# Flamingo layer with top-2 experts on one core: where the first expert tiles' rows are loaded, and three small edits around the blocks' boundary

## The reference

```python
x = x + tanh(g_xattn) * attention(layernorm(x), ctx, ctx)      # 16 heads of 16, causal
f = layernorm(x).reshape(-1, 256)
logits = f @ Wr + br                                           # 8 experts
weights = softmax(where(logits >= second_largest, logits, -inf))
h = gelu(einsum('td,edh->eth', f, W1) + b1)                    # 256 -> 1024
y = einsum('eth,ehd->etd', h, W2) + b2                         # 1024 -> 256
x = x + tanh(g_ffn) * einsum('etd,te->td', y, weights)
```

## Time and profile before

| | us |
|---|---|
| median of 3 runs | 907.57 (907.29 to 908.5) |
| the profiled execution | 904.24 |
| its span, first to last instruction | 902.5 |
| TensorE busy | 797.3 |
| first product of block 2 | 470.36 |

### The profile page before, as it was taken

How to read it: one execution, slowest core, us unless ns; L and a number is a source line. 1 busy time by engine, 2 the same in 40 slices (tenths; PEclk the granted TensorE clock), 3 DMA queues, 4 the chain that set the end, 5 groups by cost and what they waited for, 6 DMA issues and landing times. The chain is left out here.

```text
span 902.5 us, 24791 instructions
## 1 busy us (share of the span) xinstructions
PE 797.3 (88%) x7316; PEld 722.0 (80%) x7317; DVE 586.5 (65%) x1453; ACT 432.2 (48%) x955; POOL 364.3 (40%) x397
## 2 busy tenths in 40 slices
PE   3399999999999999998319999999999999999990
PEld 3289888888898888898218888888888888888880
DVE  2268999999999999988706454555545455545440
ACT  2156556665565665665105444444444444444440
POOL 2134555555565565656400233232322333332232
PEclk9699999999999999999559999999999999999996
DMA  8776887777778899984449644434333334433222
GB/s 187 135 138 123 178 177 153 135 154 157 166 162 215 198 214 222 193 172 144 146 147 295 151 70 65 65 50 64 53 56 50 53 54 56 54 51 44 25 25 27
DMA packets 132876, 108.81 MB, mean 121 GB/s; under 512 B 67744, under 2 KB 126496, under 8 KB 130592
## 3 DMA queue, kind: packets, MB, share of 16 engines
q1 hardware_dynamic: 117376, 87.19, 45.1%
q0 software_dynamic: 14304, 19.15, 13.8%
q10 hardware_dynamic: 1088, 1.11, 0.4%
HBM read 36.60 MB, written 34.36 MB: 79 GB/s over the span
## 5 line engine op out<-in xcount | busy, mean ns | idle before, releaser
L1259 POOL DMA_INDIRECT out_rows<-yg,gates x78 | 126.6, 1623 | 317.6 <-issue 150.3
L1369 PE MATMUL bank<-xh,wts 128*128 128x256 f16 x1872 | 212.2, 274 | 24.2 <-issue 24.1
L1369 PEld LDWEIGHTS bank<-xh,wts 128*128 x1872 | 183.6, 98 | 46.9 <-issue 24.9
L1385 PE MATMUL bank<-wts,hh 128*128 x1872 | 210.6, 273 | 0.0
L1385 PEld LDWEIGHTS bank<-wts,hh 128*128 128x128 f16 x1872 | 183.2, 98 | 21.2
L1285 ACT ACTIVATE hf<-bank,b1t,gscale 128x256 f32<-128x256 f32 x312 | 154.8, 562 | 20.2 <-PE bank L1369 19.1
L532 POOL TENSOR_SCALAR_AFFINE_SELECT xh<-rowmax 128x512 bf16<-128x512 bf16 x128 | 94.3, 737 | 138.3 <-DVE rowmax L785 124.0
L1036 PE MATMUL bank<-va,probs 128*128 128x102 f32 x1024 | 138.9, 277 | 9.0 <-DVE ao L733 8.9
L1316 DVE TENSOR_SCALAR hh<-hf,hscale 128x512 f16<-128x512 f32 x156 | 77.9, 499 | 104.5 <-ACT hf L1285 102.2
L1036 PEld LDWEIGHTS bank<-va,probs 128*128 128x128 f32 x1024 | 125.5, 192 | 12.1 <-DVE ao L733 6.6
L1295 ACT ACTIVATE yg<-yb,gates 128x256 f32<-128x256 f32 x78 | 35.4, 501 | 199.7 <-DVE yb L1327 148.0
(11 more groups left out here) (168 smaller groups left out, 983.9 us busy)
## 6 DMA issues: line engine op xcount, KB each, us to landing
wts<-in_W SPq DMA_DIRECT2D x16, 1024.0 KB, 6.6
wts<-keys SPq DMA_DIRECT2D x96, 128.0 KB
wts<-queries SPq DMA_DIRECT2D x96, 128.0 KB
split_weights<-wts SPq DMA_DIRECT2D x8, 1024.0 KB, 5.2
wts<-split_weights SPq DMA_DIRECT2D x8, 1024.0 KB, 7.6
xin<-in_x SPq DMA_DIRECT2D x16, 256.0 KB, 2.8
cin<-in_ctx_in SPq DMA_DIRECT2D x16, 256.0 KB, 3.6
out_rows<-x SPq DMA_DIRECT2D x16, 256.0 KB
```

The lines of the kernel that those rows point to most:

```text
L1259: pool.indirect_dma_start(out=out[:, :], out_offset=bass.IndirectOffsetOnAxis(ap=numbers, axis=0), in_=yg[m % 2][:, half, :], in_offset=No ...
L1369: last = pe.matmul(HB[c // 2][:, c % 2 * TILE:(c % 2 + 1) * TILE], wts[:, bass.ds(expert[1], 1), at:at + P], xh[(m + 1) % RING][:, xp, k, ...
L1385: last = pe.matmul(YB[b][:, half * D:(half + 1) * D], hh[b][:, hp, c, half * P:(half + 1) * P], wts[:, bass.ds(expert[0], 1), at:at + D], ...
```

## The change

- SP's waits for the table, the pads and rows_placed, and the load_rows of tiles 0 and 1, leave block 1 and stand in block 2, behind the meeting; the loads are now turns -2 and -1 of block 2's own pipeline.
- The waits for the last scatters leave GpSimd's common path (they remain in the branch for ties) and stand in SP's block 2 (rows_landed). GpSimd raises rows_placed in block 2. The semaphores `scattered` are made outside the blocks for that.
- The weights of experts 4 to 7 are read back in turns 0, 1, 2 and 3, one expert a turn, behind that turn's rows.
- ScalarE ends block 1 with a Gelu of one column whose result nobody reads.
- The last group's router products write each logit once instead of eight times.

```diff
+def rows_landed(eng, scattered):
+    for i in range(2):
+        for b in range(GT):
+            eng.wait_ge(scattered[b][i], (NG // 2) * 2 * 16)
...
         rows_placed, ties_in, row_in = sem("rows_placed"), sem("ties_in"), [sem(f"row_in{i}") for i in range(RING)]
+        scattered = [[sem(f"scattered{b}_{i}") for i in range(2)] for b in range(GT)]
...
-        scattered = [[sem(f"scattered{b}_{i}") for i in range(2)] for b in range(GT)]
+        scattered = env["scattered"]
...
                 sp.wait_ge(params, 16 * 10)
-
-                sp.wait_ge(env["table_ready"], 1)
-                sp.wait_ge(env["pads_in"], 16 * E)
-                sp.wait_ge(env["rows_placed"], 1)
-                for j in range(2):
-                    load_rows(sp, env, env["tile_row"][0:1, j:j + 1], env["first_xh"][j], j)
...
                 ties = pool.value_load(env["mostint"][0:1, 0:1], min_val=0, max_val=E)
-                for i in range(2):
-                    for b in range(GT):
-                        arrived(pool, scattered[b], NG - 2 + i, i, 2)
                 with pool.If(ties > 2):
+                    rows_landed(pool, scattered)
...
-                pool.sem_inc(env["rows_placed"], 1)
...
                 padding(act, env, range(E // 2, E))
+
+                act.activation(ex[:, 0, 0:1], lgs[:, 0, 0:1], ACT.Gelu)
...
                             for b in range(GT):
-                                last = product(PJA[:, b * MANY * E:(b + 1) * MANY * E],
+                                many = MANY if there(g) else 1
+                                last = product(PJA[:, b * MANY * E:(b * MANY + many) * E],
                                                lambda k: x2T[:, k, b * P:(b + 1) * P],
-                                               lambda k: wr[:, k, :].unsqueeze(1).to_broadcast([P, MANY, E]))
+                                               lambda k: wr[:, k, :].unsqueeze(1).to_broadcast([P, many, E]))
...
                 def it(i, m, there):
-                    if there(2) and not (isinstance(i, int) and i < 0):
+                    if there(2):
...
-                    if isinstance(i, int) and -1 <= i <= 1:
-
-                        for e in {-1: (EARLY,), 0: (EARLY + 1,), 1: range(EARLY + 2, E)}[i]:
-                            sp.wait_ge(weights_in, 16 * 2 * e)
-                            load_weights(sp, wts, w_dram, e, weights_in)
-
+                    if isinstance(i, int) and 0 <= i < E - EARLY:
+
+                        sp.wait_ge(weights_in, 16 * 2 * (EARLY + i))
+                        load_weights(sp, wts, w_dram, EARLY + i, weights_in)
+
+                sp.wait_ge(table_ready, 1)
+                sp.wait_ge(pads_in, 16 * E)
+                rows_landed(sp, scattered)
+                sp.wait_ge(rows_placed, 1)
                 all_tiles(sp, it)
...
+                pool.sem_inc(rows_placed, 1)
                 pipeline(pool, it, 0, MAIN_TILES)
```

More of the change, by code:

```diff
@@ L1171, in experts @@
         YB = [bank[5], bank[6]]
+        scattered, pads_in, table_ready, rows_placed = (
+            env[k] for k in ("scattered", "pads_in", "table_ready", "rows_placed"))
         b2_in = sem("b2_in")
```

## The result

The change makes the kernel faster: ratio to before 0.9931 (0.9904 to 0.9959), median 900.28 against 907.29 us, seven runs each in this comparison. Timed again, with new runs of both kernels, the ratio was 0.9938 (0.9912 to 0.9963). So some 6 us are gone; 3.7 were forecast.

The account below looks back on a forecast made before the run. TensorE was taken to bound the experts' block, delayed at the boundary by SP's row loads ahead of the meeting. Gains 3.6 − 0.1 + 0.2 = 3.7 us took the median 907.57 to 903.8 us, range 901.0 to 906.2.

Parts of the forecast that it names:

- Where the time is: Boundary of the blocks: SP's two tiles of loads ahead of the meeting hold TensorE; moving them starts it 3.6 us earlier.
- The DRAIN's end: GpSimd at the boundary: DRAIN ends at 457.2 to 459.0, taken as 458.1, and becomes the last to arrive.
- a length of its own: GpSimd's DRAIN at the boundary: takes 4.0 to 5.3 us whatever is in flight, so ends at 455.9 to 457.2.
- the reading tied to the landing: GpSimd's DRAIN ends 5.1 to 5.7 us behind the last landing, at 458.4 to 459.0, whatever its start.
- From DRAIN to first product: Boundary: meeting 0.2, waits 0.2, first issue 0.75, tile 0's landing 7.15, first product 0.36; sum 8.66 us.
- Tile 1: Second tile's row loads: land 6.04 us behind the first product, just in time; cost 0.1 us, ends 0 and 1.
- Router: Last group's narrower router products in block 1: gain 0.2 us, ends 0 and 1.7.
- Dummy Gelu: ScalarE's table load moved to block 1's end: hidden before and, under GpSimd's DRAIN, after; cost nothing either way.
- Weights one by one: SP's loads of experts 4 to 7, spread over turns: cost nothing, tile 4's rows leading by 7 us.
- Rival A: Boundary: the DRAIN is short and the pads' landing bounds; gain 6.4 us, 901.2 us; chance 0.18.
- B: Boundary: the DRAIN grows to 8 us or more; gain 0.2 to 1.7 us, about 906.6 us; chance 0.15.
- C: SP's single weight loads starve the tiles; slower, near 912 us at a landing of 15 us; chance 0.05.

Follow-up runs that it names:

- pool_waits: The change with GpSimd's waits for the last scatters back ahead of its branch and DRAIN; ratio to before 0.9971.
- one_tile: The change with tile 0's rows loaded ahead of the meeting again and tile 1's behind it; ratio to before 0.9927.
- no_drain: The change with both blocks closed without GpSimd's DRAIN; ratio to before 0.9887.
- no_drain_b: A repeat of the change without GpSimd's DRAIN at both block ends; ratio to before 0.9903.
- no_drain1: The change with GpSimd's DRAIN left out at the first block's end alone; ratio to before 0.9928.
- no_loads: The kernel before with single weight loads, dummy Gelu and narrow last router products, without the moved loads; ratio to before 0.9988.
- old_weights: The change with the weights read back in the old turns; one run, first to last expert product 417.9 us, 410.3 in the change.
- loads_only: The kernel before with only the row loads and waits moved behind the meeting; ratio to before 1.0031.

## Why the prediction was right, and where not

- **Where the time is.** Right: SP's loads ahead of the meeting, then GpSimd's DRAIN as the next to be last, then the pads 1 us behind that. A fell by 5.0.
- **The DRAIN's end**, the mis-sized term. I took 458.1, 19.4 us behind the mark, the middle of two readings. It ended at 18.0 (12.7 + 5.3). The reading "a length of its own" was the true one: 5295 ns in eleven profiles, with starts from 12.7 to 17.3 us behind the mark; the reading tied to the landing fell with pool_waits. That is 0.9 us of the 1.4 missing. The other 0.4 is its start: 12.7, not 13.2, 0.1 of it by the router and the rest because GpSimd went from the table to the DRAIN without its two stops.
- **From DRAIN to first product** 8.66 was forecast, 8.6 measured (26.65 − 18.04).
- **Tile 1**: 0.07 us late in the change, 0.1 forecast; 0.3 in one_tile, no_drain and no_drain_b, nothing in no_drain1, and 0.6 in pool_waits, which starts later than the change. From tile 1's first transpose to its gates SP takes 6.1 us in pool_waits, 5.6 in the change and 5.2 before; and TensorE wants the tile sooner where its stretch at 0.50 of the clock is short. The range of 0 to 1 held.
- **Router**: 0.09 measured, 0.2 taken; the pair with 8 columns was the row to believe.
- **Dummy Gelu**: hidden before and after, as said.
- **Weights one by one**, the step whose reasoning failed though the sum did not feel it. I wrote that SP's former stop "shows nowhere in the stream of products, so its removal gives nothing". Alone it gives nothing (no_loads). The new order's lead came out nearly as worked out: tile 4's rows landed 39.3 us behind tile 0's first issue (39.2 forecast), and TensorE came to its wait at 45.1 (46.3 forecast, in part because a tile takes 10.5 us and not 10.8). But I checked that lead against the new start and never asked what the old order would do to it. Its cover was a lead of zero, and with TensorE 5 us earlier each us would have shown. The edit is worth 7 to 8 us in the presence of the other (B is 417.9 and 418.5 without it, 410.3 to 411.5 with it), and without it the change is a loss.
- **Rival A** (a short DRAIN) was wrong in size, but one_tile and no_drain reached its bound from another side: the pads' landing, A at 25.3 to 25.7. **B** fell: the DRAIN, begun with scatters in flight, did not grow. **C** was the right place, SP's weight waits, with the sign of the edit turned round: it is the old bundled loads that starve the tiles, not the single ones, of which each landed in at most 9.8 us, where 12.3 was needed.
- **The number.** 5.0 us are shown in the boundary, 1.3 more than the sum's 3.7. The ratios say 5.6 to 6.3 with half an interval of 2.5; the difference is within it. The time alone would have pleaded for the wrong mechanism: 907.57 times 0.9931 is 901.3, rival A's 901.2, and it is the boundary's rows that tell the two apart. It is also close to the range's lower end of 901.0, and that end was not what I called it: A's 901.2 holds 0.2 us for the router already, and with the router's 1.7 it is 899.7.

## What to carry to other kernels

When a bound engine is to start earlier, lay its new demand times against every supplier's old delivery times; a stop that never showed may have had a lead of nothing. The small edits alone gave 0 us, the moved loads alone −3, and both together 5. Behind a barrier that one late engine hides, read the arrival of every other: the next one is the new bound. And compare two profiles from a common mark near the place in question, not from time 0.

## What the runs showed of the hardware

- GpSimd's DRAIN at the first meeting took 5295 ns in all eleven profiles that have it there, whatever was in flight (begun 12.7 to 17.3 us behind the mark, with scatters and pads moving or with neither). At the program's end it took 4017 to 4274 ns. Why the two places differ is open; quiet beside it isn't the reason, and quiet of over 0.3 us ahead of it, pads included, was not tried at the first. The 171 ns of the program's start show that it is not a price of every DRAIN. A block can be closed without it.
- After 4.3 us without a product TensorE went on at the lower clock, 0.50, and 48 products took 6.76 us (loads_only); after 3.9 us they took 7.09 (old_weights). After 1.5 and 1.4 us idle they took 5.50 and 5.43.
- Behind the boundary the granted clock stayed at 0.50 for 2.7 to 5.5 us of products, in executions of one program too (2.9 and 5.0). Half of that time is lost, and it accounts for the differences in B between kernels without gaps.
- The first block differed by 6.9 us between two profiled executions of one program (mark at 437.3 and 444.2 us), and by 9.0 over all fourteen, whose engines do the same work up to the mark (435.2 to 444.2).
